# Attention scores of a gated cross-attention layer on one core: three fp32r products of split operands, or one plain fp32 product

## The reference, cut to what matters

```python
q = l @ Wq                                   # l: normed x, 256 rows per batch
kv = jnp.concatenate([x, l], axis=1) @ Wkv   # 77 + 256 = 333 rows
k, v = jnp.split(kv, 2, axis=-1)             # 16 heads of 64
w = jnp.einsum('bhqd,bhkd->bhqk', q * scale, k * scale)
w = jax.nn.softmax(w, axis=-1)
out = jnp.einsum('bhqk,bhkd->bhqd', w, v)    # then out @ Wo
```

## Time and profile before

| | |
|---|---|
| median of 3 runs | 1330.31 us |
| lowest, highest | 1327.8, 3483.99 us |
| the profiled execution's own time | 1328.71 us |
| its span | 1327.0 us |
| mean granted TensorE clock | 0.99 |
| TensorE busy (matmul) | 1248.6 us, 94% |
| VectorE busy | 878.3 us, 66% |
| GpSimd busy | 740.0 us, 56% |
| ScalarE busy | 666.0 us, 50% |

### The profile page before, as it was taken

The page is one execution under the profiler, slowest core; times in us unless marked ns, Lnnn a source line. Parts: engine busy times, 40 slices in busy tenths (PEclk is TensorE's granted clock), DMA queues, the critical chain, the costliest instruction groups (busy, mean ns, idle before and its releaser), DMA issues.

```text
span 1327.0 us, 28196 instructions
## 1 busy us (share of the span) xinstructions
PE 1248.6 (94%) x8982; PEld 1017.4 (77%) x8982; DVE 878.3 (66%) x2646; ACT 666.0 (50%) x2022; POOL 740.0 (56%) x894
## 2 busy tenths in 40 slices
PE   3899999999999999899999998999999989999996
PEld 2688787878787878788878787878788878787774
DVE  5566677777776777777767776777766656434554
ACT  3555555555544455455544554455545566454442
POOL 2655545656664666566646665666565642344555
PEclk9999999999998999999989999999999999999998
DMA  8910000000000000000000000000000070445666
GB/s 258 314 32 1 3 1 3 17 4 18 4 17 5 17 4 18 5 18 4 17 5 17 4 18 5 17 4 18 1 17 1 17 194 29 120 126 174 186 215 207
DMA packets 61839, 70.90 MB, mean 53 GB/s; under 512 B 7072, under 2 KB 56176, under 8 KB 61680
## 3 DMA queue, kind: packets, MB, share of 16 engines
q1 hardware_dynamic: 54192, 48.91, 12.7%
q0 software_dynamic: 6912, 18.95, 4.0%
q10 hardware_dynamic: 576, 1.05, 0.2%
HBM read 35.19 MB, written 33.70 MB: 52 GB/s over the span
## 4 chain that ended last, share of the span: by engine, by line
PE 37%; POOL 29%; issue 24%; DVE 6%; DMA 2%; ACT 1%; POOLq 0%; SPq 0%; DVEq 0%; ACTq 0%
POOL probs L1108 19%; PE pj L1350 9%; PE st L560 5%; PE ov L1415 4%; PE st L1396 4%; PE st L1380 4%; POOL probs L1105 3%; POOL slots_x L982 3%; PE pj L513 3%; PE ov L579 2%; PE yb L1476 2%; POOL rstd L1088 1%; PE st L550 1%; PE pj L516 1%; DVE PT L1334 1%
## 5 line engine op out<-in xcount | busy, mean ns | idle before, releaser
L1108 POOL TENSOR_SCALAR probs<-probs,inv_sum 128x333 f32<-128x333 f32 x384 | 425.7, 1125 | 0.0
L1160 ACT ACTIVATE probs<-st,neg_max 128x333 f32<-128x333 f32 x512 | 268.8, 538 | 275.0 <-DVE neg_max L1302 275.0
L1105 POOL TENSOR_TENSOR probs<-probs,inv_sum 128x333 f32<-128x333 f32 x128 | 94.8, 741 | 407.9 <-DVE inv_sum L1313 407.7
L1302 DVE TENSOR_REDUCE neg_max<-st 128x2 f32<-128x666 f32 x256 | 205.9, 846 | 134.6 <-PE st L1396 134.6
L1380 PE MATMUL st<-ident,probs 128*128 128x128 f32 (+1 forms) x1536 | 203.8, 272 | 1.1 <-POOL probs L1108 1.1
L1415 PE MATMUL ov<-PT,V 128*64 128x256 f32 (+1 forms) x1536 | 196.9, 392 | 0.0
L1380 PEld LDWEIGHTS st<-ident,probs 128*128 128x128 f32 (+1 forms) x1536 | 182.5, 143 | 17.3 <-POOL probs L1108 1.4
L1396 PE MATMUL st<-K_hl,Q_hl 64*128 64x334 f32 x1536 | 154.1, 332 | 19.0 <-issue 9.5
L1350 PE MATMUL pj<-wkv,lT 128*128 128x512 f32 (+1 forms) x576 | 158.4, 410 | 13.4 <-DVE Q_hl L1322 13.3
L1334 DVE COPY PT<-st 128x512 f32<-128x512 f32 x256 | 163.7, 681 | 0.8 <-PE st L1380 0.8
L1186 ACT ACTIVATE V<-pj 128x512 f32<-128x512 f32 (+1 forms) x96 | 57.3, 596 | 192.8 <-PE pj L1350 192.8
(11 more groups left out here) (176 smaller groups left out, 1722.0 us busy)
## 6 DMA issues: line engine op xcount, KB each, us to landing
slots_x<-zeros SPq DMA_DIRECT2D x10, 1032.0 KB, 13.0
V<-slots_x SPq DMA_DIRECT2D x80, 129.0 KB
yg<-routed_y SPq DMA_DIRECT2D x32, 256.0 KB, 3.5
out<-X SPq DMA_DIRECT2D x32, 128.0 KB
X<-in_x SPq DMA_DIRECT2D x2, 1024.0 KB, 14.7
w_gu<-in_L_ffn_expert_gate_w SPq DMA_DIRECT2D x2, 960.0 KB, 9.1
w_gu<-in_L_ffn_expert_up_w SPq DMA_DIRECT2D x2, 960.0 KB, 10.3
w_dn<-in_L_ffn_expert_down_w SPq DMA_DIRECT2D x1, 1920.0 KB, 12.7
```

What stands on the lines that cost most here:

```text
L1105: pool.tensor_tensor(probs[:, v, 0, 0:SKV], probs[:, v, 0, 0:SKV], inv_sum[:, v, 0:1].to_broadcast([P, SKV]), ALU.mult).then_inc(normed, 1)
L1108: pool.tensor_scalar(probs[:, v, i, 0:SKV], probs[:, v, i, 0:SKV], inv_sum[:, v, i:i + 1], None, ALU.mult).then_inc(normed, 1)
L1160: nc.scalar.activation(probs[:, v, i, 0:SKV], st_bank(i)[:, 0:SKV], ACT.Exp, bias=neg_max[:, v, i:i + 1], accum_out=sums[:, v, i:i + 1]).t ...
L1302: nc.vector.tensor_reduce(neg_max[:, v, 2 * i:2 * i + 2], st[i][:, :, 0:SKV], AX.X, ALU.max, negate=True).then_inc(maxed, 1)
```

## The change

Q and K are each stored once, in plain fp32. ScalarE copies Q out of PSUM with the scale and frees the bank itself; VectorE copies K and frees its bank. The two low-part instructions of VectorE (L1322, L1327) and ScalarE's high part of K (L1180) go. The scores of a head and query tile are one plain fp32 matmul instead of three fp32r ones. Before the scores TensorE waits for the release of both banks instead of K's alone.

```diff
-    K_hl = sb("K_hl", [P, 2, 2, SKVE], F32R)
-    Q_hl = sb("Q_hl", [P, 2, 2, SQ], F32R)
+    K = sb("K", [P, 2, SKVE])
+    Q = sb("Q", [P, 2, SQ])
...
             if has(0):
-                n, bank, _, _ = filled("Q", PAIRS, bb, u)
+                n, bank, free, _ = filled("Q", PAIRS, bb, u)
                 act.wait_ge(pj_full, n + 1)
-                copy(Q_hl[:, r, 0, :], bank[:, 0:SQ], ACT.Copy, scale=SCALE).then_inc(q_hi, 1)
+                copy(Q[:, r, :], bank[:, 0:SQ], ACT.Copy, scale=SCALE).then_inc(free, 1)
...
-            if has(0):
-                n, bank, _, _ = filled("K", PAIRS, bb, u)
-                act.wait_ge(pj_full, n + 1)
-                copy(K_hl[:, r, 0, :], bank[:, 0:SKVE], ACT.Copy).then_inc(k_hi, 1)
...
             if has(0):
-                _, bank, free, _ = filled("Q", PAIRS, bb, u)
-                dve.wait_ge(q_hi, PAIRS * bb + u + 1)
-                nc.vector.scalar_tensor_tensor(Q_hl[:, r, 1, :], bank[:, 0:SQ], SCALE,
-                                               Q_hl[:, r, 0, :].bitcast(F32), ALU.mult, ALU.subtract
-                                               ).then_inc(free, 1)
-                _, bank, free, _ = filled("K", PAIRS, bb, u)
-                dve.wait_ge(k_hi, PAIRS * bb + u + 1)
-                tt(K_hl[:, r, 1, :], bank[:, 0:SKVE], K_hl[:, r, 0, :].bitcast(F32), ALU.subtract
-                   ).then_inc(free, 1)
+                n, bank, free, _ = filled("K", PAIRS, bb, u)
+                dve.wait_ge(pj_full, n + 1)
+                nc.vector.tensor_copy(K[:, r, :], bank[:, 0:SKVE]).then_inc(free, 1)
...
-                _, _, kfree, kvalue = filled("K", PAIRS, bb, u - LAG_S)
-                pe.wait_ge(kfree, kvalue + 1)
+                for kind in ("Q", "K"):
+                    _, _, free, value = filled(kind, PAIRS, bb, u - LAG_S)
+                    pe.wait_ge(free, value + 1)
...
                 for qt in range(QT):
-                    for n, (a, a_) in enumerate(((0, 0), (0, 1), (1, 0))):
-                        for head in range(2):
-                            own = slice(head * HALF, (head + 1) * HALF)
-                            last = mm(st_bank(2 * qt + head)[:, 0:SKVE], Q_hl[own, r, a, qt * P:(qt + 1) * P],
-                                      K_hl[own, r, a_, :], start=(n == 0), stop=(n == 2))
+                    for head in range(2):
+                        own = slice(head * HALF, (head + 1) * HALF)
+                        last = mm(st_bank(2 * qt + head)[:, 0:SKVE], Q[own, r, qt * P:(qt + 1) * P], K[own, r, :],
+                                  start=True, stop=True)
                     last.then_inc(st_full, 1)
```

More of the change, by code:

```diff
@@ L714, in attention @@
     pj_free = [sem(f"pj_free{i}") for i in range(len(pj))]
-    q_hi = sem("q_hi")
-    k_hi = sem("k_hi")
     st_full = sem("st_full")
```

## The result

The changed kernel takes 1331.65 us against 1328.08 us, medians of 20 runs each, a ratio of 1.0024 [1.0015, 1.0033]. That is 3.2 us slower, inside the range and inside 2%, but a third of the 9.6 us that the sum gave. (One of the runs of before took 3483.99 us; ratios leave such a run out.)

The account below looks back on a forecast made before the run. TensorE's streaming was taken as the bound, with about 20 us of waits for VectorE. Scores +26.6, V wait -12, PT copies -5 gave +9.6 us, forecast 1339 us; own range 1328 to 1352, with rivals 1325 to 1386.

Parts of the forecast that it names:

- The score block: TensorE's scores: four fp32 slots with heads side by side, 1.33 us against 1.12, 26.6 us more in 128 steps.
- No overlap: Rival, scores: fp32 passes on the two row halves shut each other out, 8 slots, 2.46 us, 1484 us; chance 0.13.
- five slots: Rival, scores: matmuls start strictly in order, 5 slots, 1.61 us a block, 1376 us; chance 0.13.
- the faster case: Rival, scores: 64-row fp32 streams as fast as fp32r, block 0.81 us, 1274 us; chance 0.04.
- 4/3 of three passes: Rival, scores: four passes, each at an fp32r pass's price, block 1.42 us, 1352 us; chance 0.08.
- The wait in front of V: TensorE before the V projection: Q's bank comes free earlier, so 12 of 13.3 us of waiting go.
- The sum itself: Whole kernel: 26.6 us for scores minus 12 before V minus 5 for PT copies, +9.6 us.
- The copies to PT: TensorE before the scores: VectorE's copies start about 0.4 us earlier, saving 5 of 6.8 us of waits.
- The chain behind the scores: Softmax after the scores: first maxima start 0.1 us later, covered by 3.8 us of slack before the transposes.
- New wait: TensorE before the scores: waiting for Q's bank costs nothing, as Q is copied about 4 us earlier.
- ScalarE: ScalarE's list: loses 0.45 us a step, 58 us in all, hidden behind TensorE; what matters is Q's bank release.
- The cold stretches: TensorE at half clock behind uncaused waits: about 3.4 us each, none or four, 7 us either way, in the range only.

Follow-up runs that it names:

- v2_plain: Kernel before with third key tile's transposes ahead of V, its copy ahead of V's on ScalarE, plus b_plain's edit: 1336.86 us, 1.0071 of the kernel before.
- b_plain: Kernel before with each score as one plain fp32 product of the high parts, low parts still made: 1343.6 us, 1.0111 of the kernel before.
- a_heads: Changed kernel with score products reordered, both query tiles of head 0, then both of head 1: 1346.2 us, 1.0131 of the kernel before.

## Why the prediction was right and where it failed

**The score block: right.** 4 slots of 282 ns and 0.20 us of ends were forecast, 1.33 us; 1.324 was measured, 1.330 with the heads in the other order. Its 26.2 us are paid nearly in full only where little waits (v2_plain, 25.0). The nearest row, the product with V, was the right one: halving by columns told what halving by rows would do. No overlap, five slots and the faster case are out; so is 4/3 of three passes (1.42 us).

**The wait in front of V: right in kind, too small.** This is the step that failed. I took 12 of the 13.3 us that the profile lists as idle time of the matmuls; the blocks ahead of V lost 20.7 us. The list holds only the waits that outlast the matmuls in flight, 27 of 94. In others the bank came free about 0.1 us too late for V's first weight load, and I read those steps as waiting for nothing because no idle time was marked. The page had the right size, 20.3 us in the row of V's weight loads, and I did not read that row.

**The sum itself: the terms were not independent.** I charged 26.6 us for the block and credited the waits as if each came apart. b_plain shows that the longer block alone, with all of VectorE's work in place, got 11.5 us back, about 3 of them perhaps the clock's. The other 11.5 us came with K's copy, Q's low part and the release. Together 23 us came back instead of the 17 forecast. By the traces it is 20.7 in front of V and 6.2 in front of the scores, less the 2.8 us by which step 3 grew outside the score block: 24.

**The copies to PT: right by the traces.** I took 5 us; the block that had held the wait got 6.2 us shorter, 4.5 of it with K's single copy. The runs alone are too coarse to show that part (1.2 us, up to 4.0).

**The chain behind the scores: wrong in one step of eight.** I followed it to the transposes alone and found 3.8 us of slack. Through GpSimd's scatter and VectorE's list it also leads to the routing products of step 3, and there VectorE's low part was done only 0.15 us ahead of them (median) in the kernel before. The sum has no term for this wait, which cost 2.8 us.

**New wait, ScalarE, GpSimd's work: right.** No wait for Q before the scores, GpSimd's part 739 us as before, ScalarE's 54 us less without an effect of its own that any run shows, beyond the release, and VectorE's 41 us less felt only in what TensorE waits for. The cold stretches lay within the 7 us allowed.

That the time lies inside the range has some luck in it. The credit in front of V was 8.7 us too small, and 4.5 us that the sum did not have, of step 3 and of half clock, came in on the other side.

## What to carry to other kernels

Before pricing a longer or shorter block on the bounding engine, look at what the next blocks wait for and when it came free: where a wait ends just before a block starts, extra time in front of it is partly free (14.7 us for 26.2 here, some of it the clock's) and saved time is partly lost (30 us gained for 79). The matmuls' listed idle time is a lower bound for such a wait, since a late release also holds back the weight load without any idle matmul; read the weight loads' row too (20.3 us against 13.3 here, 20.7 gained). Then follow the second engine's list to every place where the first waits for it: time won ahead of V in step 2 came back as a wait in step 3, behind a DMA. The remedy that worked here was to move the waiting block behind one that waits for nothing, and to move its consumers' copies in the same order on the other engines; moving only one of the two cost 15 us here, moving both gained 16.

## What the runs showed of the hardware

- Plain fp32 on row halves of the array runs two heads side by side: 8 instructions of 64 rows and 334 columns in a block of 1.324 us, also with four in a row for the same half (1.33 us, a_heads). There head 1's products started ahead of head 0's later ones, and their report still came last: 1.42 us for an instruction that starts at 0.40. An instruction's duration rose from 332 ns in fp32r to 478 ns (means).
- A weight load held back by a late semaphore cost about 0.1 us in a step (0.885 against 0.790 us for eight transposes) without showing as idle time of the matmuls; it shows as idle time of the weight loads.
- Behind the loop's turns, where TensorE stood still for up to 2.5 us before and 2.7 us in the changed kernel (four waits, 9.5 and 9.2 us in all), its clock fell to 1.2 GHz for 3.4 or 6.8 us, in some turns and not in others.
